# Softmax sums of two attention layers: ones' matmuls once per group, the key tiles added on GpSimd

## The reference, cut to what matters

```python
q, k, v = ...                                    # 4 batches, 16 heads, 512 rows, 32 columns
p = jax.nn.softmax(q @ k.T * 32**-0.5, axis=-1)  # cross attention: scores above the diagonal masked
o = p @ v
x = x + o.reshape(4, 512, 512) @ w_o.T
```

## Time and profile before

| | |
|---|---|
| median of 3 runs | 2966.02 us |
| the profiled execution | 2973.69 us |
| its span, first to last instruction | 2971.9 us |
| mean granted clock of TensorE | 0.908 of full speed |
| TensorE busy (matmuls) | 2490.0 us, 84% of the span |
| VectorE busy | 1772.6 us, 60% |
| ScalarE busy | 1224.7 us, 41% |
| GpSimd busy | 800.9 us, 27% |

### The profile page before, as it was taken

One profiled execution on the slowest core, in us unless ns is written; L12 is line 12 of the kernel. 1 busy time (PEld: TensorE's weight loads), 2 busy tenths in 40 slices (PEclk: granted clock), 3 DMA queues, 4 the chain that ended last, 5 costly groups with the idle time before them and its releaser, 6 DMA issues. The chain is left out here.

```text
span 2971.9 us, 34593 instructions
## 1 busy us (share of the span) xinstructions
PE 2490.0 (84%) x12822; PEld 1649.0 (55%) x12822; DVE 1772.6 (60%) x2762; ACT 1224.7 (41%) x1859; POOL 800.9 (27%) x1064
## 2 busy tenths in 40 slices
PE   5898999884443458998759999999999879999999
PEld 4554545421222247888645554545555548888887
DVE  3766666545799967777636555655565444444443
ACT  3343434335766725455314333443433223333332
POOL 2222222213567546788600000001211110000000
PEclk8999999986665678999979999999999889999999
DMA  3213132202222347999733322333433331101000
GB/s 112 73 44 86 44 86 47 68 15 93 89 93 79 120 172 214 267 266 266 192 95 72 88 77 73 96 91 99 125 90 92 115 118 74 43 1 43 1 29 15
DMA packets 177017, 287.09 MB, mean 97 GB/s; under 512 B 20769, under 2 KB 52385, under 8 KB 176866
## 3 DMA queue, kind: packets, MB, share of 16 engines
q1 hardware_dynamic: 159458, 249.73, 28.6%
q0 software_dynamic: 14336, 34.61, 5.4%
q10 hardware_dynamic: 3072, 0.79, 0.1%
HBM read 149.79 MB, written 58.98 MB: 70 GB/s over the span
## 5 line engine op out<-in xcount | busy, mean ns | idle before, releaser
L657 DVE TENSOR_REDUCE at_negmax<-at_ps 128x2 f32<-128x1024 f32 (+3 forms) x256 | 259.3, 1018 | 131.5 <-PE at_ps L420 66.7
L572 ACT ACTIVATE at_probs<-at_ps 128x1024 f32<-128x1024 f32 (+3 forms) x256 | 221.7, 866 | 265.5 <-PE at_ps L440 262.6
L1258 DVE TENSOR_REDUCE a_negmax<-a_ps 128x2 f32<-128x1024 f32 x128 | 155.2, 1217 | 140.4 <-PE a_ps L1011 139.8
L50 PE MATMUL ff_ps<-ff_xnT_hi,ff_s_hi 128*128 128x512 f32 x512 | 201.0, 393 | 5.1 <-DVE ff_xnT_lo L2769 5.1
L52 PE MATMUL ff_ps<-ff_xnT_hi,ff_s_lo 128*128 128x512 f32 x512 | 200.2, 391 | 0.0
L51 PE MATMUL ff_ps<-ff_xnT_lo,ff_s_hi 128*128 128x512 f32 x512 | 200.2, 391 | 0.0
L1159 ACT ACTIVATE a_probs<-a_ps 128x1024 f32<-128x1024 f32 x128 | 130.9, 1023 | 139.8 <-PE a_ps L1029 139.3
L1842 ACT ACTIVATE gr_act_signs<-gr_signed,gr_test 128x512 bf16<-128x512 f32 x248 | 177.3, 717 | 25.4 <-POOL gr_test L2207 11.0
L440 PE MATMUL at_ps<-at_qk 98*128 98x512 f32 (+3 forms) x512 | 171.8, 418 | 17.6 <-DMA at_qk<-at_mrow 10.9
L2799 DVE TENSOR_TENSOR ff_hid<-ff_hid,ff_ps 128x512 f32<-128x512 f32 x64 | 44.0, 688 | 238.8 <-ACT ff_hid L2744 238.8
L440 PEld LDWEIGHTS at_ps<-at_qk 98*128 98x128 f32 x512 | 83.1, 193 | 158.8 <-issue 90.0
(11 more groups left out here) (413 smaller groups left out, 6428.9 us busy)
## 6 DMA issues: line engine op xcount, KB each, us to landing
at_qk<-at_part SPq DMA_DIRECT2D x384, 128.0 KB, 2.4
first_gu<-in_L_ffn_w_gate_up_dram SPq DMA_DIRECT2D x32, 1024.0 KB, 6.3
a_qk<-a_part SPq DMA_DIRECT2D x192, 128.0 KB, 2.3
first_d<-in_L_ffn_w_down_dram SPq DMA_DIRECT2D x32, 512.0 KB, 8.3
gr_aside_raw<-in_L_ffn_W_dram SPq DMA_DIRECT2D x48, 256.0 KB, 3.4
w13T<-gr_aside_out SPq DMA_DIRECT2D x32, 256.0 KB, 3.3
shared_x<-x_after_cross SPq DMA_DIRECT2D x8, 1024.0 KB, 7.8
ff_slab<-w13T SPq DMA_DIRECT2D x14, 512.0 KB, 6.4
```

Of the source, the lines that this page charges most:

```text
L50: pe.matmul(out, lh, rh, start=start, stop=False, skip_group_check=True)
L572: act.activation(probs[:, t % 2, 2 * w:2 * w + 2, lo:S], banks(("kq", g, s), lo), ACT.Exp, scale=SCALE).then_inc(free(("kq", g, s)), 1)
L657: dve.reduce_max(negmax[:, g % 2, :].rearrange("p (j t) -> p j t", t=NT)[:, 2 * w:2 * w + 2, t], banks(("qk", g, s), 0, width(g, t)), AX.X ...
L1258: dve.reduce_max(negmax[:, g % 2, :].rearrange("p (j t) -> p j t", t=NT)[:, 2 * w:2 * w + 2, t], banks(("qk", g, s)), AX.X, negate=True).t ...
```

## The change

The ones' pass runs once per group, at its end, over the full width, on the sum of the four key tiles' exponentials (`add_up(g)`). That sum is made by GpSimd: `fold(g, t, w)` adds the half w of tile t onto the half w of tile 0, in place, for t = 1 to 3. A fold into tile 0 waits until the value pass over tile 0 has read it.

The buffer of two tiles, `probs`, becomes five half buffers of two heads each (`both_of`): three for w=0 and two for w=1; the fifth is a third of `got`. An exponential of tiles 2 and 3 waits for the value pass and the fold of the tile that used its half before. As `got[:, 2]` holds exponentials to the end, the second weight chunk of the network (`load_chunk(1)`) is loaded after the loop, when sums and products of all groups are done; the first one is loaded where it was. The normalization of the group before stands on GpSimd behind the sixth slot's fold.

```diff
-        probs = sb("probs", [P, 2, QUAD, S])
+        halves = sb("halves", [P, 4, 2, S])
...
+        folded = [sem(f"folded{w}") for w in range(2)]
...
+        def both_of(g, t, w):
+            i = ((0, 1, 2, 1)[t] - g) % 3 if w == 0 else 3 + (g + (t > 0)) % 2
+            return halves[:, i] if i < 4 else got[:, 2]
...
@@ SP
-                for k in range(FF_AHEAD):
-                    sp.dma_start(ff_chunk(got, None, k)[:, 0:2, :], ...).then_inc(ff_in, 16)
-                    sp.dma_start(ff_chunk(got, None, k)[:, 2, :], ...).then_inc(ff_in, 16)
+                load_chunk(0)
...
+            sp.wait_ge(sums_done, G)
+            sp.wait_ge(values_done, NT * G)
+            for k in range(1, FF_AHEAD):
+                load_chunk(k)
             sp.wait_ge(res_out, 16 * (2 * ALL - 1))
             sp.wait_ge(ff_in, 16 * 2 * FF_AHEAD)
@@ TensorE
-            def add_up(g, t):
-                lo = first(g, t)
-                if t == 0 and g >= 1:
+            def add_up(g):
+                if g >= 1:
                     pe.wait_ge(sums_out, g)
+                for w in range(2):
+                    pe.wait_ge(folded[w], (NT - 1) * (g + 1))
                 for j in range(QUAD):
-                    mm = pe.matmul(ps[j * HD:(j + 1) * HD, SUMS, lo:S], ones[:], probs[:, t % 2, j, lo:S],
-                                   start=t == 0, stop=t == NT - 1, skip_group_check=True)
+                    mm = pe.matmul(ps[j * HD:(j + 1) * HD, SUMS, :], ones[:], probs_of(g, 0, j), start=True, stop=True, skip_group_check=True)
...
-                else:
-                    add_up(g, n // 2)
+                elif n == PAIRS - 1:
+                    add_up(g)
@@ ScalarE, exponentials(g, s)
-                if NT * g + t >= 2:
-                    act.wait_ge(sums_done, NT * g + t - 1)
+                if t == 0 and g:
+                    act.wait_ge(values_done, NT * g - (1, 0)[w])
+                    act.wait_ge(folded[w], (NT - 1) * g - (1, 0)[w])
+                if t == 1 and g:
+                    act.wait_ge(sums_done, g)
+                if t == 3 or (t, w) == (2, 1):
+                    old = t - 2 + w
+                    act.wait_ge(values_done, NT * g + old + 1)
+                    act.wait_ge(folded[w], (NT - 1) * g + old)
@@ GpSimd
+            def fold(g, t, w):
+                lo = first(g, t)
+                if causal(g):
+                    pool.wait_ge(masked, PAIRS * (g - NC * B) + 2 * t + w + 1)
+                else:
+                    wait_drained(pool, "kq", g, 2 * t + w)
+                if t == 1:
+                    if not causal(g):
+                        wait_drained(pool, "kq", g, w)
+                    pool.wait_ge(values_done, NT * g + 1)
+                else:
+                    pool.wait_ge(folded[w], (NT - 1) * g + t - 1)
+                total, part_of = both_of(g, 0, w)[:, :, lo:S], both_of(g, t, w)[:, :, lo:S]
+                pool.tensor_tensor(total, total, part_of, ALU.add).then_inc(folded[w], 1)
...
+                for s in range(PAIRS if has(g) else 0):
+                    if causal(g):
+                        mask_diagonal(g, s)
+                    if s >= 2:
+                        fold(g, s // 2, s % 2)
+                    if s == NORMALIZE_AT:        # 6
+                        normalize(g - 1)
```

More of the change, by code:

```diff
@@ L320, in first, with probs_of @@
             return t * P if causal(g) else 0
+        def both_of(g, t, w):
+            i = ((0, 1, 2, 1)[t] - g) % 3 if w == 0 else 3 + (g + (t > 0)) % 2
+            return halves[:, i] if i < 4 else got[:, 2]
+        def probs_of(g, t, j):
+            return both_of(g, t, j // 2)[:, j % 2, :]
         def width(g, t):
@@ L371, in load_for_network, with load_chunk @@
                 sp.wait_ge(mask_ready, 1)
-                for k in range(FF_AHEAD):
-                    sp.dma_start(ff_chunk(got, None, k)[:, 0:2, :], w13T.rearrange("(k p) (m e) -> k p m e", p=P, m=2)[k]).then_inc(ff_in, 16)
-                    sp.dma_start(ff_chunk(got, None, k)[:, 2, :], w2_mixed.rearrange("(k p) d -> k p d", p=P)[k]).then_inc(ff_in, 16)
+                load_chunk(0)
+            def load_chunk(k):
+                sp.dma_start(ff_chunk(got, None, k)[:, 0:2, :], w13T.rearrange("(k p) (m e) -> k p m e", p=P, m=2)[k]).then_inc(ff_in, 16)
+                sp.dma_start(ff_chunk(got, None, k)[:, 2, :], w2_mixed.rearrange("(k p) d -> k p d", p=P)[k]).then_inc(ff_in, 16)
             load(sp, 0)
@@ L453, in weigh @@
                 for j in range(QUAD):
-                    mm = pe.matmul(ps[j * HD:(j + 1) * HD, NUM, lo:S], v[:, g // NC % 2, t, c * P + j * HD:c * P + (j + 1) * HD], probs[:, t % 2, j, lo:S],
+                    mm = pe.matmul(ps[j * HD:(j + 1) * HD, NUM, lo:S], v[:, g // NC % 2, t, c * P + j * HD:c * P + (j + 1) * HD], probs_of(g, t, j)[:, lo:S],
                                    start=t == 0, stop=t == NT - 1, skip_group_check=True)
                 mm.then_inc(values_done, 1)
-            def add_up(g, t):
-                lo = first(g, t)
-                if t == 0 and g >= 1:
+            def add_up(g):
+                if g >= 1:
                     pe.wait_ge(sums_out, g)
+                for w in range(2):
+                    pe.wait_ge(folded[w], (NT - 1) * (g + 1))
                 for j in range(QUAD):
-                    mm = pe.matmul(ps[j * HD:(j + 1) * HD, SUMS, lo:S], ones[:], probs[:, t % 2, j, lo:S],
-                                   start=t == 0, stop=t == NT - 1, skip_group_check=True)
+                    mm = pe.matmul(ps[j * HD:(j + 1) * HD, SUMS, :], ones[:], probs_of(g, 0, j), start=True, stop=True, skip_group_check=True)
                 mm.then_inc(sums_done, 1)
@@ L569, in exponentials @@
                 act.wait_ge(kq_ready, PAIRS * g + s + 1)
-                if NT * g + t >= 2:
-                    act.wait_ge(sums_done, NT * g + t - 1)
-                act.activation(probs[:, t % 2, 2 * w:2 * w + 2, lo:S], banks(("kq", g, s), lo), ACT.Exp, scale=SCALE
+                if t == 0 and g:
[7 more added lines that the diff above has]
+                    act.wait_ge(folded[w], (NT - 1) * g + old)
+                act.activation(both_of(g, t, w)[:, :, lo:S], banks(("kq", g, s), lo), ACT.Exp, scale=SCALE
                                ).then_inc(free(("kq", g, s)), 1)
@@ L605, in _ @@
                     if s == 1 and has(g - 1):
-                        act.wait_ge(sums_done, NT * g)
+                        act.wait_ge(sums_done, g)
                         act.copy(weighed[:, 1, :], ps[:, SUMS, :]).then_inc(sums_out, 1)
@@ L748, in mask_diagonal, with normalize @@
                 wait_drained(pool, "kq", g, s)
-                diagonal = probs[:, t % 2, 2 * w:2 * w + 2, t * P:(t + 1) * P]
+                diagonal = both_of(g, t, w)[:, :, t * P:(t + 1) * P]
                 pool.affine_select(out=diagonal, in_=diagonal, compare_op=ALU.is_ge, fill=0.0, base=0,
                                    pattern=[[0, 2], [1, P]], channel_multiplier=-1).then_inc(masked, 1)
+            def fold(g, t, w):
[12 more added lines that the diff above has]
+                pool.tensor_tensor(total, total, part_of, ALU.add).then_inc(folded[w], 1)
+            def normalize(g):
+                if not has(g):
+                    return
+                pool.wait_ge(rec_done, NT * (g + 1))
+                if g >= NC:
+                    pool.wait_ge(y_ready, 2 * (g // NC))
+                pool.tensor_tensor(oT[:, g % NC, :], weighed[:, 0, :], weighed[:, 1, :], ALU.mult).then_inc(o_done, 1)
+            NORMALIZE_AT = 6
             rstds(0)
@@ L759, in _ @@
                                        pattern=[[-1, P]], channel_multiplier=1).then_inc(masks_made, 1)
-                for s in range(PAIRS if has(g) and causal(g) else 0):
-                    mask_diagonal(g, s)
-                if has(g - 1):
-                    pool.wait_ge(rec_done, NT * g)
-                    if g - 1 >= NC:
-                        pool.wait_ge(y_ready, 2 * ((g - 1) // NC))
-                    pool.tensor_tensor(oT[:, (g - 1) % NC, :], weighed[:, 0, :], weighed[:, 1, :], ALU.mult).then_inc(o_done, 1)
+                for s in range(PAIRS if has(g) else 0):
[5 more added lines that the diff above has]
+                        normalize(g - 1)
+                if not has(g):
+                    normalize(g - 1)
                 if g % NC == 0 and 1 <= g // NC + 1 < ALL:
```

## The result

The changed kernel takes 3024.74 us (median of 4 runs, 3019.25 to 3028.59), the kernel before beside it 2965.72 (4 runs): ratio 1.0195, 95% interval 1.0178 to 1.0213. It is slower, as forecast, but by 59 us where the sum gave 31.6. The profiled execution after has a span of 3017.5 us at a mean granted clock of 0.896, before 2971.9 at 0.908.

The account below looks back on a forecast made before the run. TensorE was nearly always busy in both attention layers, but VectorE ended some steps. Second attention +13.6, cross attention +10.0, last batch -1.5, layer end +4.0 and hand-over +5.5 gave +31.6: 2998 us (own range 2980 to 3020; 8 in 10: 2952 to 3030).

Parts of the forecast that it names:

- The layernorm meets the folds: Second attention, c=1 (group mod 4): layernorm pieces and folds take turns, so the second output product comes 5.95 us later.
- The chain that ends c=0: First step of a batch: VectorE's reduction, reciprocal and statistic, 2.53 us a slot, end it; removed passes gain 0.
- The passes of slots 3 and 5: Of three passes removed per step, only these can shorten it: 1.8 us each in second attention's c=2 and c=3.
- The load at the hand-over: After the last store, SP waits for the network's second weight chunk: +5.5 us, bounds +3.5 and +9.
- GpSimd at the layer's end: In the last group nothing hides folds, masks and normalization on GpSimd: +4.0 us, bounds +2 and +6.
- the one on slot 7: Slot 7's ones' pass, before the maxima's transpose, is covered by VectorE's last reduction; removing it gains 0.
- the new gaps of c=1: TensorE's idle time there lowers its clock: 1.9 us a step in second attention, 1.3 in cross attention.
- rival C: Longer waits before the transposes lower the clock in most steps: another 20 steps at 1.3 us, 3024; chance 0.15.
- the cross attention's c=1: Output product 4.0 us late, less 0.79 for slot 5's pass: +3.2, and 1.3 for the clock, per batch.
- Rival A: Layernorm in c=1 isn't held up by folds, or VectorE keeps its turn: 2952 to 2959 us; chance 0.20.
- Rival B: TensorE stays the bound everywhere and all removed passes count: 75 us less, 2891; chance 0.05.
- The price that the forecast took from the earlier trace: Cross attention: a projection behind waits for VectorE ran at clock 0.54, against 1.00 next step: 1.3 us lost.

Follow-up runs that it names:

- experiment 1: Changed kernel; in c=1 (group mod 4 = 1) the first fold also waits until the four layernorm pieces are done: 3005.4 us, 1.0131.
- experiment 2: Changed kernel with the four layernorm pieces of c=1 in slot 1 in place of slot 2: 2975.6 us, 1.0035.
- experiment 3: Changed kernel with folds of the last column alone, all waits kept: 2968.6 us, 1.0013.
- experiment 12: Changed kernel with each fold issued as two operations of half the size: 3021.0 us, 1.0186.
- experiment 8: Changed kernel with folds in the second attention alone, second chunk loaded early, layernorm in slot 1, c=0's row statistics in slots 0, 1, 6 and 7: 2947.8 us, 0.9939.
- experiment 5: Kernel before, with the ones' pass of slot 7 (key tile 2) one column wide: 2977.0 us, 1.0053.
- experiment 6: Kernel before, with the ones' passes of key tiles 0 to 2 one column wide and no folds: 2960.6 us, 0.9983.
- experiment 9: The kernel of experiment 8 plus 1.0 us of useless TensorE work in slot 7 of each second-attention step: 2938.3 us, 0.9907.
- experiment 4: Kernel before, with only the load of the network's second weight chunk moved behind the loop: 2971.5 us, 1.0020.
- experiment 11: Changed kernel with the useless TensorE pass in slot 7 of the second attention's steps, nothing else moved: 3011.6 us, 1.0150.

## Why the prediction was right and wrong

**Right.** The layernorm meets the folds, and they take turns: 6.06 us of waiting against 5.95, the pieces long as the folds, the output product slowed by 2.1 against 1.9; experiments 1, 2, 3 and 12 each change that wait as the mechanism says. By the Trainium skill, page "SBUF — State Buffer", section "SBUF: two separate sides", the later of the two engines stands still until the other's instruction is over; the trace agrees (2.57 us for a piece of 0.5 alone), and experiment 12 adds that the other is served after each one. The chain that ends c=0: the second attention's first such step in full swing went from 23.73 to 23.74, and experiment 8 moved it. The passes of slots 3 and 5: c=3 of the second attention gained 1.9 to 2.2 in three of four steps (forecast 1.8). The load at the hand-over: 4.9 in the trace and 5.1 alone, against 5.5. GpSimd at the layer's end: 4.4 by experiment 3, against 4.0.

**Wrong in size: the clock.** The step that failed is the one on slot 7: the pass is covered, "So of three passes removed from a step only those of slots 3 and 5 can shorten it". It doesn't shorten the step, true, but that was taken to mean that its removal costs nothing, and experiment 5 prices it at +10.7 us. The pass filled a wait for VectorE, and kept TensorE's clock up. The forecast charged the clock to the new gaps of c=1 alone (4 x 1.9 + 3 x 1.3 = 11.5 us); the longer waits before the transposes were left to rival C, at 0.15. The six output products behind the gaps lost 12.1 us together (1.6 to 2.5 each), so that charge was about right. The projections' 23.6 us come on top of it. With C's 26 us added, the sum was 3024, and the measurement is 3024.7: forecast and C were not alternatives but two parts of one result. That they meet within a microsecond is luck: C had 20 steps at 1.3 us, the trace has 17 stretched projections, and other terms missed by a few us both ways. The forecast's own range (2980 to 3020) misses the result; the wider one holds it only because it reached to C.

**Wrong in the cross attention's c=1**: counted from the transpose, the second output product came 3.1 us later than before (22.51 against 19.40 us in group 21; 2.52 of it waiting), not 4.0. The clock cost more: 1.9 a step in that product and 0.4 in the projection, on average, against 1.3. So the sum of the term, +15.8 against +13.5, came out near by two errors.

**Rival A** falls: no piece runs at 0.5 us while folds are queued. **Rival B** falls with experiments 5 and 6.

What stays open: which waits bring the clock down. In c=0 and c=3 of the second attention waits of 1.15 and 1.32 us were followed by a projection at 1.00 (but for group 12 of the changed kernel); waits of 1.32 in c=1 (experiment 8) and of 1.36 in c=2 (experiment 5) were followed by stretched ones, and there another wait of about 1 us had gone just before. One projection of experiment 9 was stretched behind a wait of 0.53. The price that the forecast took from the earlier trace rows doesn't belong to the wait alone either: the slow projection there stands behind a wait of 0.80, the fast one behind 0.75. Nor does a longer gap always cost more: behind the 3.78 us of experiment 12 two output products took 10.1 us, behind 6.06 in the changed kernel 8.9 to 9.5. And in part it is a matter of the execution: in the trace of experiment 4, whose loop is that of the kernel before, three projections are stretched too, but those of groups 2, 18 and 26 in place of 17, 22 and 26. The runs show that filling the waits removes nearly all of the stretching in the second attention, not the rule.

## What to carry to other kernels

Before work is taken off an engine, look at what it covers: where the next step waits for another engine anyway, the removed work comes back as idle time, and here TensorE's idle time cost a lower clock in what followed, more than the work was worth; even a useless product paid. Before work is put on GpSimd, look which VectorE operations beside it are held up (here the layernorm pieces alone), and move one of the two by a slot. Read step lengths by their position in the loop, since a sum over the layer hides that c=2 and c=3 gained while c=1 lost.

## What the runs showed of the hardware

GpSimd loses little by the turns: a fold that lets one VectorE piece through takes 2.52 to 2.54 us and not 2.37, while the piece takes 2.57 and not 0.5. Not every VectorE operation is held up: in the second attention of the changed kernel 53 reciprocals (SBUF to SBUF) that ran beside a fold took 0.93 to 0.95 us, 16 row statistics 0.63 to 0.69, and the reductions of 128x1024 from PSUM 1.15 to 1.23, all as in the kernel before; only the layernorm pieces were longer.

In stretches of six microseconds from a projection's start the granted clock was 1.00, 0.72 or 0.50 in the rows shown. In the changed kernel one projection behind a removed pass of 1.0 us took 2.7 us longer (8.64 against 5.94, group 10); with the useless pass in its place it took 5.94 again (experiment 11).
